# Spreading the loads for the attention's first group over the third batch of the projection stage

## The reference, cut to what matters

```python
xn = layernorm(x)                                  # x: [4, 1024, 256]
qkv = (xn @ W_qkv + b_qkv)                         # 16 heads of 16
q, k = rope(q), rope(k)
attn = softmax(q @ k.T * 16 ** -0.5)               # per batch and head
y = (attn @ v) @ W_out + b_out
w, idx = top-4 of 16 experts in 2 of 4 groups by sigmoid(xn @ w_gate.T)
routed = sum over the 4 chosen experts of w * (silu(xn @ w1.T) * (xn @ w3.T)) @ w2.T
shared = (silu(xn @ w1_s.T) * (xn @ w3_s.T)) @ w2_s.T
out = x + y + routed + shared
```

## Time and profile before

| | before |
|---|---|
| median of 3 runs | 1234.71 us (1231.74 to 1236.12) |
| profiled execution: device time | 1240.19 us |
| profiled execution: span, first to last instruction | 1238.2 us |
| mean granted TensorE clock | 0.962 |
| PE / DVE / ACT / POOL busy share of the span | 94% / 78% / 61% / 47% |
| stage a (to stage b's first DMA issue) | 0 to 176.4 us |
| DMA, mean over the span | 147 GB/s |

### The profile page before, as it was taken

One profiled execution on the slowest core, in us unless ns is written; L12 is line 12 of the kernel. 1 busy time (PEld: TensorE's weight loads), 2 busy tenths in 40 slices (PEclk: granted clock), 3 DMA queues, 4 the chain that ended last, 5 costly groups with the idle time before them and its releaser, 6 DMA issues. The chain is left out here.

```text
span 1238.2 us, 27841 instructions
## 1 busy us (share of the span) xinstructions
PE 1168.3 (94%) x8338; PEld 585.0 (47%) x8339; DVE 960.1 (78%) x1450; ACT 752.9 (61%) x1568; POOL 580.5 (47%) x861
## 2 busy tenths in 40 slices
PE   4996969999999999999999999998999999998998
PEld 2553533333333333333333333333788887774665
DVE  6464658699999999999999999980555555555888
ACT  3653522688888888888888888887333333330000
POOL 6995966444556563232313232331566666660000
PEclk9998975799999999999999999999999999998999
DMA  7465653526354433434233332402677666644775
GB/s 218 133 199 190 214 142 131 194 61 189 98 144 127 141 115 96 116 91 98 78 105 102 100 88 80 110 29 68 198 225 229 210 197 214 198 154 157 234 225 174
DMA packets 127000, 181.74 MB, mean 147 GB/s; under 512 B 41153, under 2 KB 88641, under 8 KB 124994
## 3 DMA queue, kind: packets, MB, share of 16 engines
q1 hardware_dynamic: 111554, 138.55, 38.6%
q0 software_dynamic: 15360, 42.04, 9.7%
HBM read 99.71 MB, written 80.81 MB: 146 GB/s over the span
## 5 line engine op out<-in xcount | busy, mean ns | idle before, releaser
L1048 DVE TENSOR_REDUCE mx<-pm 128x1 f32<-128x1024 f32 x512 | 621.1, 1222 | 27.5 <-PE pm L1098 26.9
L1022 ACT ACTIVATE pr<-pst 128x512 f32<-128x512 f32 x1024 | 556.6, 596 | 84.4 <-PE pst L1109 32.3
L1098 PE MATMUL pm<-kt,qt 48*128 48x512 f32 x1024 | 389.0, 463 | 14.1 <-PEq L141 7.2
L1109 PE MATMUL pst<-qt,kt 50*128 50x512 f32 x1024 | 380.2, 451 | 0.0
L1121 PE MATMUL po<-pr,vt 128*17 128x256 f32 x4096 | 325.0, 390 | 9.7 <-ACT osb L1032 9.3
L1098 PEld LDWEIGHTS pm<-kt,qt 48*128 48x128 f32 x1024 | 158.1, 193 | 239.9 <-DVE mx L1048 175.7
L1268 POOL DMA_INDIRECT s_y<-ys_c,slot_c x144 | 139.8, 971 | 86.3 <-issue 49.5
L1121 PEld LDWEIGHTS po<-pr,vt 128*17 128x17 f32 x4096 | 69.0, 95 | 200.0 <-issue 112.5
L1109 PEld LDWEIGHTS pst<-qt,kt 50*128 50x128 f32 x1024 | 153.9, 187 | 12.3 <-ACT pr L1022 10.9
L950 POOL DMA_INDIRECT s_xg<-p_rows,p_slot x128 | 125.4, 980 | 56.0 <-issue 30.2
L1345 PE MATMUL c_pG<-w13s,xt_c 128*128 x576 | 150.2, 384 | 0.1
(11 more groups left out here) (187 smaller groups left out, 1182.0 us busy)
## 6 DMA issues: line engine op xcount, KB each, us to landing
xg<-s_xg SPq DMA_DIRECT2D x144, 128.5 KB
yg<-s_y SPq DMA_DIRECT2D x32, 512.0 KB, 4.0
s_q<-stg SPq DMA_DIRECT2D x32, 256.0 KB
s_k<-stg SPq DMA_DIRECT2D x32, 256.0 KB
kt<-s_k SPq DMA_DIRECT2D x32, 256.0 KB
qt<-s_q SPq DMA_DIRECT2D x64, 128.0 KB
s_o<-osb SPq DMA_DIRECT2D x32, 256.0 KB, 7.0
w13s<-w SPq DMA_DIRECT2D x1, 4608.0 KB, 14.4
```

What stands on the lines that cost most here:

```text
L1022: nc.scalar.activation(pr[:, (k % 2) * 4 + ORDER[i], :], pst[bank(gg, k, i)][:, :], ACT.Exp, scale=SCALE).then_inc(exp_ok, 1)
L1048: nc.vector.tensor_reduce(mx[:, half, col:col + 1], pm[slot][:, :, :].rearrange("p a n -> p (a n)"), AX.X, ALU.max).then_inc(mx_free, 1)
L1098: mm = pe.matmul(pm[slot][:, kk, :], qt[buf][rows, half, pair, qi * P:(qi + 1) * P], kt[buf][rows, pair, kk * 512:(kk + 1) * 512], start=T ...
L1109: pe.matmul(pst[bank(buf, k, i)][:, :], kt[buf][rows, pair, kc * P:(kc + 1) * P], qt[buf][rows, half, pair, :], start=True, stop=True)\
```

## The change

The 13 DMAs of `first_loads` are the same, with the same sources, destinations and semaphores, but are issued at several steps. With n counted from step 16: at n = 0 and 2 the two DMAs of one band of the keys, at n = 4 and 6 the two of one band of the first half of the queries, at n = 8 and 10 the same of the second half, and at n = 12 the values. The waits for batch 0's stores stay at n = 0.

```diff
             def first_loads(k, t, b):
-                if k == 2 * TPB:
+                n = k - 2 * TPB
+                if n == 0:
                     for i in range(2):
                         sp.wait_ge(st_out[i], STORES * 16)
                     for i in range(TPB):
                         sp.wait_ge(v_out[i], 16)
-                    load_keys(sp, s_k, first["kt"][0], 0, first["qk_in"])
-                    load_queries(sp, s_q, first["qt"], 0, 0, first["qk_in"])
-                    load_queries(sp, s_q, first["qt"], 1, 0, first["late_in"])
+                if n in (0, 2):
+                    load_keys(sp, s_k, first["kt"][0], 0, first["qk_in"], (n // 2,))
+                if n in (4, 6):
+                    load_queries(sp, s_q, first["qt"], 0, 0, first["qk_in"], (n // 2 - 2,))
+                if n in (8, 10):
+                    load_queries(sp, s_q, first["qt"], 1, 0, first["late_in"], (n // 2 - 4,))
+                if n == 12:
                     load_values(sp, s_v, first["vt"], 0, 0, first["v_in"])
...
-def load_rows_of(eng, src, dst, runs, gi, done):
+def load_rows_of(eng, src, dst, runs, gi, done, pars=(0, 1)):
-    for par in range(2):
+    for par in pars:
...
-def load_keys(eng, s_k, kt, gi, done):
-    load_rows_of(eng, s_k, kt, K_RUNS, gi, done)
+def load_keys(eng, s_k, kt, gi, done, pars=(0, 1)):
+    load_rows_of(eng, s_k, kt, K_RUNS, gi, done, pars)
-def load_queries(eng, s_q, qt, half, gi, done):
-    load_rows_of(eng, s_q[half], qt[:, half, :, :], Q_RUNS, gi, done)
+def load_queries(eng, s_q, qt, half, gi, done, pars=(0, 1)):
+    load_rows_of(eng, s_q[half], qt[:, half, :, :], Q_RUNS, gi, done, pars)
```

## The result

| | before | after |
|---|---|---|
| median of 20 runs | 1233.85 us (1230.13 to 1240.19) | 1231.02 us (1225.7 to 1234.45) |
| ratio, after to before | | 0.997, 95% interval 0.9958 to 0.9982 |
| profiled execution: span | 1238.2 us | 1223.7 us |
| stage b's first DMA issue | 176.37 us | 172.41 us |

The change makes the kernel 2.8 us faster; 3.4 were forecast.

A forecast was written before the change was run, and what follows sets the result against it. Bound: ACT's stall on late stores, worth 12.2 us, then engines 0 and 1 at 61.6 us over three periods. Release 163.1 - 160.2 = 2.9, plus 0.5, gives 3.4: 1234.7 - 3.4 = 1231.3 us; 8 in 10 from 1225 to 1237.

The forecast's parts named there:

- The first wait: ACT's `part1` at tile 16: the 13.14 us wait for stores goes, barely, with step 17's stores beginning at 84.5.
- The waits come back at tiles 20, 24 and 28: ACT in stage a: waits of 3.1, 4.8 and 4.2 us, where they were 0.28, 0.71 and 1.64.
- The engines' sum: DMA engines 0 and 1, per period between store sets: 15.8 us plus loads, making 20.4, 21.4, 19.8; 61.6 in all.
- SP's sums: SP's queue, per period between store sets: 17.3 us plus issue of its loads, making 19.4, 19.6 and 19.0.
- The Trainium skill's rule: DMA engines consume descriptors in ring order, so loads cost the same wherever they stand; without it, gain towards 12.2 us.
- ACT's arrivals: ACT in stage a: comes to tiles 20, 24 and 28 at 115.9, 135.6 and 156.0 us.
- The tail: From tile 28's release to stage b: the path stays, 13.2 us then and now.
- The 0.5 us: End of stage a: TensorE, ahead of a waiting ACT, has the last projections ready; added to the 2.9 us gain.
- What was put at nothing: Later landing of loads, ACT's other store waits, and TensorE's clock with 0 to 1 us idle each: no cost.
- The full gain: Rival in stage a: the stall goes and nothing takes its place, 12.2 us, 1222.5; chance 0.11.
- The slower rival: SP's hold belongs to the values, costing up to 7.3 us at step 28: 1237.4 us; chance 0.15.
- The second bound: SP's queue in stage a: if only its issues counted, three periods make 58.0 us and the gain is 6.5.

The follow-up runs named there:

- e4: Kernel before with all 13 first-group loads issued behind the last set of big stores (steps 30 to 33): 1223.24 us, ratio 0.9911.
- e1: Kernel before with the first group's four broadcast query loads each split into two plain 16-row loads: 1227.68 us, ratio 0.9948.
- e3: Kernel before with only the values moved to step 28, keys and queries staying at step 16: 1232.29 us, ratio 0.9992.
- e2: Changed kernel with the first group's four broadcast query loads each split into two plain 16-row loads: 1226.62 us, ratio 0.9949.
- e5: Changed kernel with all eight query DMAs at step 20 instead of 20, 22, 24 and 26: ratio 1.0082, in a slow set at 1400 us.
- e8: Kernel before with first-group loads behind the last big stores and broadcast query loads split in all 16 groups: 1219.7 us, ratio 0.9886 in its last set.
- e6: Kernel before with all first-group loads behind the last big stores, values ahead of the keys at step 30: ratio 0.9963, time not told apart.

## Why the prediction was right

**The first wait goes.** Right: the first set was forecast at 84.5 and stands at 83.40 + 0.68 = 84.1; tile 16 waits for nothing.

**The waits come back at tiles 20, 24 and 28.** Right, and this is the result: 13.1 us of waiting went, and 11.9 came back. Releases were forecast at 119.0, 140.4 and 160.2; with the 0.68 they are 118.2, 139.9 and 159.9. e4 shows that it is the loads ahead of the sets that bring them: without those, 0.4 us is left of all four.

**The engines' sum bounds each period.** Right for the landings, and right in the total of the periods, 61.9 measured for 61.6; but off one by one, 19.5, 20.0, 22.4 for 20.4, 21.4, 19.8, so that the total fits so well is partly luck. The first two periods are SP's sums (19.4 and 19.6): SP ran ahead, and the two engines' backlog shows at the releases. The last small store ahead of the sets of steps 21 and 25 has 14 of its 16 increments by 105.06 and 124.20 and all of them only at 107.28 and 127.95; the releases follow 10.3 and 11.2 us later, 14.7 and 16.3 us after the sets began and not 14.1. In the third period SP itself was held: the queries of step 26 took 2.1 us to issue and not 1.2, and the store behind the values 2.2 and not 0.4, together 2.8 of the 3.4 us above SP's sum of 19.0. Its set was released 14.0 us after its start. That the queries' two engines are among the stores' eight was called an assumption; e1, e3 and the increments bear it out.

**The Trainium skill's rule** ("DMA: Bandwidth & Descriptors", "Queues, rings and completion order") that each DMA engine takes its descriptors in ring order agrees with e3: 7.6 us earlier at the issue made 1.3 us at the landing, and the small stores behind the queries were complete on 14 of 16 increments 9 us before the last two.

**ACT's arrivals** were put too late. I had it come to tile 24 16.6 us after the release before, as in the earlier trace rows; it came after 14.5 (139.19 - 7.19 - 117.55); I take the reason to be that a wait of 2.4 us had hardly set it back. So its waits sum to 14.6 and not 12.1. That cost nothing, as the release is set by the stores.

**The tail**, 13.2 us from the last release to stage b, is 172.41 - 159.26 = 13.15. The 0.5 us I added for a TensorE that is ahead did come and was lost again. The exponential follows the release by 1.5 us where it was 2.4, and VectorE starts on the rows of tile 29 2.3 us behind the release (161.56) where it was 3.2. Then it runs almost without a gap to its end, but its first routing instruction (`g_sc` from `g_ex`) takes 0.97 us where it took 0.22. It lay under a POOL instruction (161.78 to 163.05) and ended 0.08 us after it; it is the same in e1 and e2 (0.96) and e5 (0.61), each ending 0.08 to 0.09 us after POOL's. Where POOL's had less than 0.1 us to run or had not begun (before, e3, e4, e8) it took 0.22.

**What was put at nothing.** TensorE was to idle 0 to 1 us behind ACT's new waits. It idled 4.2 us from 130 to 140 us, and behind that the granted clock was 0.83 from 140 to 150. The releases came on time all the same, as the prediction had it for that case.

**The rivals.** The full gain was ruled out for this placing and is real for another: e4 has 10.3 us, e8 14.0. The slower rival put the hold on the values. It was half right on the hold, which needs the values (e3) and queued queries ahead of them (e1, e6), and wrong on what it costs: at step 28 it was 2.2 us with one band of queries before it, and 0.65 in e3 and e5, where none stood there. My argument against it, that it ended as the queries drained, was the other half of the matter. No hold stood behind the queries at steps 20 and 22; behind the stores' tail at step 26 their issue itself took 2.1 us. The second bound, SP's own issuing, was in the prediction as the lower sum (58.0); e2 shows it, at 60.3 with four more DMAs in those periods, and the first two periods of the changed kernel follow it. The two bounds lie so close that relieving the engines alone gains little here.

## What to carry to other kernels

A load that has no use yet costs its engines' work to whatever stands behind it in their queues; spreading it over the loop moves that cost and saves little if those engines, or the queue that issues to them, are nearly full. Look for the place where nothing waits behind it (here after the last set of stores, 10 us) before thinning it out (3 us), and for a shape that uses more engines (6 us with no load moved). And look at how many engines a DMA uses: a broadcast over an outer dimension of two put 128 KB on two of 16, and a DMA share of 0.12 beside a stalled queue is how it looks in the windows.

## What the runs showed of the hardware

- A DMA whose source is broadcast over an outer dimension of two sits on two of the 16 engines: DMA share 0.12 to 0.13 at 49 to 53 GB/s, and behind it small stores with 14 of 16 increments in and the last two up to 9 us later (e3). Split into plain loads of 16 rows, all 16 come within 0.4 us (e1).
- The point at which SP is held and the point at which time is lost are different things: 7.3 us of hold moved the landing by 1.3 us (e3).
- A DMA of many short runs holds SP when its engines already have a queue: 7.3 us behind eight query loads, 6.15 and 6.39 in e4's two traces, 2.2 after, 0.65 when the queries are split (e8) or long done (e3), none to see right behind it when no queries are queued (e6).
- VectorE's `g_sc` instruction took 0.96 to 0.97 us (0.61 in e5) under a POOL instruction that ran on and 0.22 otherwise, and in the first case ended 0.08 to 0.09 us after POOL's; no run here tests what makes it wait.
- Two profiled executions with the same stage b differ by 7 us in one stretch of it (82.9 against 75.9) with the granted clock at 1.2 GHz for some 17 us in it where the other stayed at 2.4, which is twice the effect that was to be measured.
